# Eight router tiles transposed by DMA instead of TensorE, and router and rank matmuls moved inside the block, in a graph layer with a mixture of experts

## The reference

```python
x = x + gnn(layernorm(x), edges, W, b)           # out[i] = sum over edges of dis[i]*dis[j]*h[j], h = x W^T + b
flat   = layernorm(x)                            # 1250 x 1024
logits = flat @ router_w.T + router_b            # 1250 x 8
top2   = top_k(logits, 2); wt = softmax(top2 values)
out    = sum over e of wt[e] * (gelu(flat @ w1[e].T + b1[e]) @ w2[e].T + b2[e])
x      = x + layernorm(out + flat) * ln_w + ln_b
```

## Time and profile before

| | |
|---|---|
| median of 3 runs | 638.55 us (638.48 to 639.12) |
| the profiled execution | 635.89 us |
| its span, first to last instruction | 634.2 us |
| TensorE busy | 544.2 us, 86% |
| VectorE busy | 475.1 us, 75% |
| ScalarE busy | 231.5 us, 37% |
| GpSimd busy | 202.5 us, 32% |

### The profile page before, as it was taken

The page is one execution under the profiler, slowest core; times in us unless marked ns, Lnnn a source line. Parts: engine busy times, 40 slices in busy tenths (PEclk is TensorE's granted clock), DMA queues, the critical chain, the costliest instruction groups (busy, mean ns, idle before and its releaser), DMA issues.

```text
span 634.2 us, 12301 instructions
## 1 busy us (share of the span) xinstructions
PE 544.2 (86%) x3660; PEld 299.3 (47%) x3661; DVE 475.1 (75%) x1295; ACT 231.5 (37%) x348; POOL 202.5 (32%) x198
## 2 busy tenths in 40 slices
PE   1598999999999999999399899999999999999200
PEld 0243444444444455555376565656565655565100
DVE  8899976885408589898886869686867676765297
ACT  4232332223207133434544433444343443411470
POOL 2750000000000135656653443525344544151230
PEclk9989999999989999999589999999999999999755
DMA  5596123333214624434656987878897969163979
GB/s 214 185 388 232 35 46 66 51 59 57 55 35 151 247 118 143 174 136 166 203 173 227 268 269 168 267 202 263 229 267 194 290 178 297 43 144 102 252 212 278
DMA packets 59565, 112.34 MB, mean 177 GB/s; under 512 B 33490, under 2 KB 33903, under 8 KB 59504
## 3 DMA queue, kind: packets, MB, share of 16 engines
q1 hardware_dynamic: 49424, 80.02, 36.9%
q0 software_dynamic: 8896, 27.38, 20.7%
q10 hardware_dynamic: 1184, 4.20, 1.8%
HBM read 71.75 MB, written 33.67 MB: 166 GB/s over the span
## 4 chain that ended last, share of the span: by engine, by line
PE 67%; DVE 20%; DMA 5%; issue 4%; ACT 2%; DVEq 1%; POOL 1%; POOLq 0%; ACTq 0%; SPq 0%
PE ps L1775 7%; PE ps L1776 6%; PE ps L1894 6%; PE ps L1895 6%; PE ps L1896 6%; PE ps L1873 5%; PE ps L1875 5%; PE ps L1874 5%; PE ps L1855 4%; PE ps L1697 4%; PE ps L1698 3%; PE ps L1699 3%; DVE wbufs L1169 3%; DVE wbufs L1168 2%; PE ps L1639 2%
## 5 line engine op out<-in xcount | busy, mean ns | idle before, releaser
L605 POOL DMA_INDIRECT acc_rows<-work,ids_out x24 | 53.0, 2208 | 104.5 <-DVE work L1492 104.5
L518 POOL TENSOR_TENSOR work<-work 128x1024 f16<-128x1024 f32 x9 | 19.2, 2130 | 208.2 <-ACT work L890 208.2
L1873 PE MATMUL ps<-rows_and_counts,wbufs 128*128 128x336 f16 (+2 forms) x256 | 74.9, 298 | 3.1 <-issue 2.3
L1775 PE MATMUL ps<-wbufs,rows_and_counts 128*128 128x512 f16 x200 | 75.8, 379 | 0.5 <-DVE wbufs L1274 0.5
L1776 PE MATMUL ps<-wbufs,rows_and_counts 128*128 128x512 f16 x200 | 75.8, 379 | 0.0
L1874 PE MATMUL ps<-rows_and_counts,wbufs 128*128 128x336 f16 (+2 forms) x256 | 74.8, 298 | 0.0
L1875 PE MATMUL ps<-rows_and_counts,wbufs 128*128 128x336 f16 (+2 forms) x256 | 74.8, 298 | 0.0
L1447 DVE SCALAR_TENSOR_TENSOR wbufs<-stage,wbufs 128x1024 f16<-128x1024 f32 x56 | 67.2, 1219 | 9.5 <-ACT wbufs L917 9.5
L1894 PE MATMUL ps<-wbufs,rows_and_counts 128*128 (+1 forms) x192 | 72.8, 379 | 1.5 <-issue 1.3
L1895 PE MATMUL ps<-wbufs,rows_and_counts 128*128 (+1 forms) x192 | 72.8, 379 | 0.0
L1896 PE MATMUL ps<-wbufs,rows_and_counts 128*128 (+1 forms) x192 | 72.8, 379 | 0.0
(11 more groups left out here) (305 smaller groups left out, 1063.6 us busy)
## 6 DMA issues: line engine op xcount, KB each, us to landing
stage<-wst_in SPq DMA_DIRECT2D x72, 512.0 KB, 6.1
acc_rows<-work SPq DMA_DIRECT2D x10, 512.0 KB, 3.2
x_rows<-work SPq DMA_DIRECT2D x10, 512.0 KB, 2.7
t<-x_in SPq DMA_DIRECT2D x1, 4096.0 KB, 14.2
wbufs<-b_in ACTq DMA_DIRECT2D x8, 512.0 KB, 5.8
wbufs<-acc_rows SPq DMA_DIRECT2D x8, 512.0 KB, 6.2
t<-x_in SPq DMA_DIRECT2D x1, 3072.0 KB, 11.9
t<-x_in SPq DMA_DIRECT2D x1, 2048.0 KB, 7.7
```

The costliest lines, as they stand in the source:

```text
L1775: mm(o, ct_hi[:, cs], hs[:, at:at + HALF], start=(m == 0), stop=False, skip_group_check=True)
L1873: mm(o, wbufs[:, ds(w + ws, P)], x_hi, start=(j == 0), stop=False)
```

## The change

Tiles 0 to 7 (`BY_DMA = 8`) are no longer transposed by TensorE. SP issues one transposing DMA from `xs` into `x2t` for each, between the two stores to HBM, after `route(r-1)` has read `x2t`. So `turn2`, ACT's copy and `x2t_lo` are left for tiles 8 and 9 alone. ACT may overwrite `xs` only after the transposing DMA has landed, and `route` waits for it. On TensorE's queue `route(r-2)` moves from between the halves to the middle of the second half, and `rank(r-3)` stands between the halves where `rank(r-2)` stood behind the block; from `r = 9` on `rank(r-2)` is also done behind the block.

```diff
+BY_DMA = NT - 2
 ...
@@ SP, for each tile r, after the store of xn and the wait for xs
+                if r < BY_DMA:
+                    sp.wait_ge(router_done, r)
+                    sp.dma_start_transpose(x2t.rearrange("p (b k) -> p b k", k=P), xs).then_inc(x2t_in, 16)
                 sp.dma_start(x2_rows[rows, :], xs.bitcast(F32)).then_inc(x2_first_stored if r < FIRST_TILES else x2_stored, 16)
@@ ACT
-                if r >= 1:
-                    act.wait_ge(x2t_done, r)
+                if r > BY_DMA:
+                    act.wait_ge(x2t_done, r - BY_DMA)
                     act.wait_ge(router_done, r - 1)
                     a.activation(x2t[:, 0:D], x2t_ps, ACT.Copy).then_inc(x2t_hi_done, 1)
                 if r < NT:
                     sqrt_var(r)
                     act.wait_ge(xn_done, NT + r + 1)
-                    act.wait_ge(x2t_done, r)
+                    act.wait_ge(x2t_in, 16 * min(r, BY_DMA))
+                    act.wait_ge(x2t_done, max(r - BY_DMA, 0))
                     stored(act, r)
                     a.activation(xs[:, 0:D], xn, ACT.Copy).then_inc(xs_hi_done, 1)
@@ DVE, add_agg
-                if 1 <= r < NT - 1:
+                if BY_DMA < r < NT - 1:
                     x2t_lo(r - 1)
@@ TensorE, aggregate: now over a range of the ten source tiles
-            def aggregate(r, n):
+            def aggregate(r, n, blocks=range(NT)):
-                for m in range(NT):
+                for m in blocks:
...
+                if blocks[-1] < NT - 1:
+                    return
@@ TensorE, route
-                pe.wait_ge(x2t_lo_done, r + 1)
+                pe.wait_ge(x2t_in, 16 * min(r + 1, BY_DMA))
+                pe.wait_ge(x2t_lo_done, max(r + 1 - BY_DMA, 0))
@@ TensorE, the loop
             for r in range(NT + 2):
                 if r < NT:
                     aggregate(r, 0)
+                    if r >= 3:
+                        rank(r - 3)
+                    aggregate(r, 1, range(NT // 2))
                 if r >= 2:
                     route(r - 2)
                 if r < NT:
-                    aggregate(r, 1)
-                if 1 <= r <= NT:
+                    aggregate(r, 1, range(NT // 2, NT))
+                if BY_DMA < r <= NT:
                     turn2(r - 1)
                 if r == NT + 1:
                     for j in range(2):
                         turn_first(j, FIRST).then_inc(first_done, 1)
-                if r >= 2:
+                if r >= NT - 1:
                     rank(r - 2)
```

More of the change, by code:

```diff
@@ L410, in build @@
         x2_stored = sem("x2_stored")
+        x2t_in = sem("x2t_in")
         x2t_done = sem("x2t_done")
@@ L1288, in x2t_lo @@
             def x2t_lo(r):
-                dve.wait_ge(x2t_hi_done, r + 1)
+                dve.wait_ge(x2t_hi_done, r - BY_DMA + 1)
                 v.tensor_tensor(x2t[:, D:], x2t_ps, x2t[:, 0:D], ALU.subtract).then_inc(x2t_lo_done, 1)
@@ L1785, in turn2 @@
                 pe.wait_ge(xs_done, NT + r + 1)
-                pe.wait_ge(x2t_lo_done, r)
+                pe.wait_ge(x2t_lo_done, r - BY_DMA)
                 transposed(x2t_ps, xs).then_inc(x2t_done, 1)
             def route(r):
-                pe.wait_ge(x2t_lo_done, r + 1)
+                pe.wait_ge(x2t_in, 16 * min(r + 1, BY_DMA))
+                pe.wait_ge(x2t_lo_done, max(r + 1 - BY_DMA, 0))
                 pe.wait_ge(mask_done, 2 * r)
```

## The result

The kernel before took 637.36 us (median of 20 runs, 635.22 to 639.41), the changed kernel 639.39 (20 runs, 637.29 to 641.59). The ratio is 1.003, with an interval of 1.0018 to 1.0042: **slower by 2.0 us, some 0.3%**. 636.1 had been forecast, 2.4 faster. The 638.55 that the forecast started from was the median of three of these 20 runs, so the forecast is best read as a difference. The profiled execution went from 635.89 to 638.43, its span from 634.2 to 636.8.

The account below looks back on a forecast made before the run. TensorE's matmul queue was taken as the bound, shifting to a store loop of 9.8 + 0.2 = 10.0 us; tile 9 2.4 us earlier, so 638.55 - 2.4 = 636.1 us, range 631.5 to 643.

Parts of the forecast that it names:

- What bounds the kernel before: In the blocks, up to 300 us, TensorE's matmul queue sets the pace, at 10.34 us a block.
- the sum of removed matmuls: TensorE's queue loses 8 x 16 matmuls, 8 x 0.89 = 7.1 us, all before the end of block 9.
- What is moved costs nothing: `route` and `rank` at new places on TensorE's queue cost their old 0.7 us; second add 0.7 late at most.
- The bound moves to the loop `xn`, ACT, POOL, transposing DMA, store: Per tile, this loop takes 10.0 us, above TensorE's 9.45 and DVE's 8.95, so most of 7.1 isn't won.
- TensorE's waits before `route`: TensorE no longer busy throughout the blocks, idle before `route` from block 7 on; 1.1 us idle at `route(7)`.
- The store follows the transposition without waiting for its landing: On SP's queue, the store's packets stand right behind the transposition's: loop 9.8 us rather than 11.3.
- Tile 9 8.95 behind tile 8, the rest rigid: DVE's own queue sets the last step, 8.95 us; `xn` of tile 9 comes 2.4 earlier, and the end follows.
- Loop: 4.14 + 3.7 + 1.3 + 0.6 + 0.06 for the wake = 9.8 us: `xn` to SP's issue 4.14, transposing DMA 3.7, store's packets 1.3, their landing 0.6, wake 0.06.
- and add 0.2: Allowance on the 9.8 us loop for landings whose mean is above their median; gives 10.0 us.
- The break-even: Loop of 10.30 us, or store landing 6.1 after the transposing DMA's issue, where the change stops paying.
- The rival on the slower side: DVE's wait in `stored`: store begins only after the transposition lands, loop 11.3, 8.0 later, 646.5 us; chance 0.22.

Follow-up runs that it names:

- Experiment 5: Changed kernel with two `xs` buffers in turn and a separate semaphore for the store of `xn`, which alone DVE awaits: 630.39 us, ratio 0.9893 to the kernel before.
- experiment 3: Changed kernel with `BY_DMA = 0`: only the moves of `route` and `rank`, all tiles transposed by TensorE; 635.28 us, ratio 0.9994 to the kernel before.
- experiment 9: Changed kernel with 94 semaphore increments at the head of TensorE's queue, shifting its instruction fetches; 647.17 us, ratio 1.013 to the kernel before.
- Experiment 10: Changed kernel with POOL's scatters of tiles 0 to 6 held back and issued together after tile 8; one run, 651.1 us, total not comparable.
- experiment 8: Changed kernel with two `xs` buffers and POOL's scatters moved behind its split of a weight piece; 637.19 us, ratio 0.9994 to the kernel before.

## Why the prediction was wrong

Point by point, in its own order.

- **What bounds the kernel before**: right. Experiment 5 won back 7.15 of the 7.1 us that the sum of removed matmuls gave.
- **What is moved costs nothing**: right (experiment 3).
- **The bound moves to the loop `xn`, ACT, POOL, transposing DMA, store**: right, in place and in kind. Waits before the writing of `xn`, ended by the store, were named beforehand, and there are eight. TensorE's waits before `route` were named too, from block 7 on; they came for tiles 3 to 6 (1.1, 0.8, 0.5 and 2.2 us) and not for tile 7.
- **The store follows the transposition without waiting for its landing**: right. In tile 0 it lands 5.6 us after the transposing DMA's issue; waiting for the landing would give 4.4 + 2.7 = 7.1. The Trainium skill's "DMA: Bandwidth & Descriptors", "Queues, rings and completion order", had said so, and the trace agrees.
- **Tile 9 8.95 behind tile 8, the rest rigid**: right (8.93; 2.1 us at tile 9, 2.0 in the medians).
- **The failed step is the size of one term**: "Loop: 4.14 + 3.7 + 1.3 + 0.6 + 0.06 for the wake = 9.8 us", and then "and add 0.2". The measured mean is 10.58. Of the 0.78 above the sum, 6.26 - 5.6 = 0.66 is the store's landing, and the rest the wake, 0.18 in the mean instead of 0.06. The way from `xn` to SP's issue, 4.14, was right (4.24 for tile 0, 4.13 or 4.14 for the others). Tiles 0 and 1, whose transfers nothing crosses, took 10.03 and 9.84: the value taken was that of an undisturbed tile. Over eight tiles the landings exceed 5.6 by 5.3 us in all: 3.7 of it in tiles 2 and 6, with instruction packets in the transposition; 0.9 in tiles 4, 5 and 7, where scatters run beside it; 0.8 in tile 3, where scatters, a short instruction packet and a store issued 0.44 late by SP (250.66 instead of 250.22) come together.

The break-even had been worked out as a loop of 10.30, or a store landing 6.1 us after the transposing DMA's issue. Measured were 10.58 and 6.26, and 8 x (10.58 - 10.30) = 2.2 us slower is what came. So the sign was decided by 0.28 us a tile, where the sum was off by 0.78, and with the allowance of 0.2 still by 0.58. The rival on the slower side decided, by its point of decision; its mechanism, a store that waits for the landing, is not what happens. The allowance named two rows. The one of stage 1, 4.3 to 4.7, was taken where, in the earlier trace rows, nothing runs beside the transposition. The one that warned was the other: landings of 2.6 to 7.0 for the store. The 7.0 is tile 9's, behind the blocks; within them the latest were 4.9 (tile 3) and 3.1. With 3.4 us to spare such a delay cost nothing; in a loop without slack each one is paid in full.

The chance of 0.22 for slower was not small, and the range held the time. The wrong part was to give a loop whose slack I had just computed as gone the landings of an undisturbed transfer plus 0.2.

**What stays open.** That an instruction packet makes the transposition late is shown by its moving along in experiment 9 and by its absence in short landings; it was not tried with the packets alone, since their time can't be set directly. Which engine's code queue 14 carries is not settled. What the changed kernel would take without the packets is only an estimate: with tiles 2 and 6 at some 10.2, near their neighbours, 12.00 + 11.51 - 20.4 = 3.1 us less, some 1 us under the kernel before.

## What to carry to other kernels

Work taken from the bounding engine pays only down to the next loop of waits: write out that loop link by link, ask for each buffer which transfer its next writer really waits for, and give it its own semaphore, or a second buffer, before the work is moved (here 0.9928 and 0.9893 instead of 1.003). A transfer's landing in a loop without slack counts with its mean, late ones included, and with the late ones of the stretch where it will stand; where the forecast's sign hangs on less than the spread of the landing, the forecast is "unclear". And before a helper engine's instructions are put back to back, look at what operations of its neighbour slip between them.

## What the runs showed of the hardware

**A transposing DMA all but stops while an instruction packet is served beside it.** DMA throughput of the changed kernel, tile 0 undisturbed (216 to 224 us, slices of 0.2), then tile 2 (237 to 242, slices of 0.125), with the instruction packets of that stretch:

```profile
GB/s 0 0 0 0 0 0 0 0 12 186 216 215 212 210 216 220 218 214 216 191 210 334 448 410 369 451 451 225 21 0 0 0 0 0 0 0 0 0 0 0
```

```profile
GB/s 0 0 0 131 80 207 213 195 197 109 92 0 0 16 8 10 10 8 150 276 276 209 8 6 8 8 8 6 88 285 287 293 293 289 295 287 577 525 131 393
...
q14 instruction: 1, 0.01, 1.7%
q8 instruction: 1, 0.02, 1.5%
```

Undisturbed, it moves some 215 GB/s for 2.6 us, and the store follows at once at some 370 to 450. In tile 2 there are two holes of some 0.8 us, in which at most 16 GB/s are left, about what one of 16 engines would move of 215 (13.4) or less; after the second it runs at 285 to 295, and the store waits. The trace's records of single packets go with it. A transposition is 2048 packets of 256 bytes, which take 0.018 us in the median. In tile 2, 39 of them stay open for 0.87 to 1.28 us, across the holes; in tile 6, 21 for 0.44 to 0.77; in tiles 0, 1, 3, 4, 5 and 7, none for more than 0.2. That looks as if one of the 16 engines, held by an instruction packet, lets the other fifteen wait and then catches up. This is inferred, since the records don't say which engine served a packet. Experiment 9, tile 4 (272 to 274.5 us, slices of 0.0625), has the same picture with one packet (20 packets open for 1.01 to 1.35 us):

```profile
GB/s 193 164 152 139 238 184 221 213 197 233 205 238 209 213 233 451 209 197 205 188 127 94 119 123 106 57 16 4 4 8 4 8 8 12 8 8 8 12 12 4
...
q8 instruction: 1, 0.02, 2.2%
```

Experiment 10, tile 5 (267 to 275 us, slices of 0.2), has neither scatters nor instruction packets, and no hole:

```profile
GB/s 0 0 0 0 0 0 152 219 215 211 212 215 214 220 216 218 196 204 414 392 471 410 410 348 246 143 123 164 287 287 266 307 369 164 123 143 123 82 410 328
```

**The order of the two DMAs matters.** Store, then transposition: it lands 5.1 to 7.5 us after its issue instead of 4.3 to 6.1 (without tiles 2 and 6, 5.1 to 6.2 instead of 4.3 to 4.9), and holds SP's queue for 3.2 to 3.8 us instead of 1.3 to 2.1.

**Some small DVE operations wait for whole POOL instructions.** The two one-hot operations on 8 elements a partition took 0.36 us together in experiment 5 and 2.19 in experiment 8, and between two POOL instructions with no gap they didn't get in. Others do not wait: in the same rows `MAX8` and the one behind it took 0.17 and 0.21 us while POOL's first instruction ran. The Trainium skill's "SBUF — State Buffer", section "SBUF: two separate sides", describes the ports that the two share as an exclusive lock for a whole instruction, which a DVE operation needs in a two-port mode or with two inputs in SBUF. The trace agrees on the lock, with 1.21 and 2.19 us against 0.24 and 0.36; which mode an operation ran in, no row shows.
